# The second four tiles of a batch summed by ScalarE's accumulator in two of four periods

## What is computed

```python
cos = einsum('bhsd,bhtd->bhst', q, k)           # q, k with length 1
g = arccos(clip(cos, -1 + EPS, 1 - EPS))
score = (1 + g) ** -3.2
n_r, n_c = score.sum(-1), score.sum(-2)
k_tilde = score / n_r[..., None] / n_c[..., None, :]
out = (k_tilde / max(k_tilde.sum(-1), 1e-12)) @ v
```

## Time and profile before

| | us |
|---|---|
| median of 3 runs | 5188.83 (5183.14 to 5189.67) |
| the profiled execution | 5182.72 |
| its span, first to last instruction | 5181.0 |
| VectorE busy | 4095.3 |
| ScalarE busy | 4828.4 |
| TensorE busy | 3096.4 |
| GpSimd busy | 1904.3 |

### The profile page before, as it was taken

How to read it: one execution, slowest core, us unless ns; L and a number is a source line. 1 busy time by engine, 2 the same in 40 slices (tenths; PEclk the granted TensorE clock), 3 DMA queues, 4 the chain that set the end, 5 groups by cost and what they waited for, 6 DMA issues and landing times.

```text
span 5181.0 us, 37309 instructions
## 1 busy us (share of the span) xinstructions
PE 3096.4 (60%) x10590; PEld 798.7 (15%) x10590; DVE 4095.3 (79%) x4051; ACT 4828.4 (93%) x1248; POOL 1904.3 (37%) x629
## 2 busy tenths in 40 slices
PE   7555555555465545654566655665655565565799
PEld 4200111111010000100011111111111111111344
DVE  8777787877777777877788888888888888888577
ACT  5899999999999999999999999999999999999621
POOL 4433444334433444334433343334424442344000
PEclk9776657666766676567667778686877878787799
DMA  3100000000000000000000101010100101010200
GB/s 97 61 10 14 17 19 19 13 11 18 18 15 18 11 11 10 10 2 10 12 30 29 33 27 37 10 45 10 41 22 24 37 22 41 2 53 2 83 32 13
DMA packets 72049, 128.21 MB, mean 25 GB/s; under 512 B 9750, under 2 KB 47269, under 8 KB 71909
## 3 DMA queue, kind: packets, MB, share of 16 engines
q1 hardware_dynamic: 70757, 122.55, 7.6%
q0 software_dynamic: 1152, 4.19, 0.3%
HBM read 96.72 MB, written 29.88 MB: 24 GB/s over the span
## 4 chain that ended last, share of the span: by engine, by line
ACT 56%; issue 22%; DVE 11%; PE 7%; DVEq 1%; ACTq 0%; DMA 0%; SPq 0%
ACT X L1332 14%; ACT X L1305 13%; ACT X L1316 10%; ACT X L1324 9%; ACT X L1345 7%; DVE X L1092 4%; DVE ncol L1100 3%; PE psum L1561 3%; DVE rows L1197 1%; ACT L1316 1%; PE psum L959 1%; PE psum L974 1%; PE psum L933 1%; DVE X L1078 1%; PE psum L1526 0%
## 5 line engine op out<-in xcount | busy, mean ns | idle before, releaser
L1278 POOL TENSOR_TENSOR X<-X 128x2048 f32<-128x2048 f32 x504 | 1798.4, 3604 | 2803.0 <-DVE X L1078 2803.0
L933 PE MATMUL psum<-stacks 128*128 128x512 bf16 x4096 | 1672.0, 502 | 807.9 <-DVE X L1092 422.1
L1092 DVE TENSOR_TENSOR X<-psum,X 128x1024 f32<-128x1024 f32 x1024 | 1191.7, 1218 | 419.4 <-ACT X L1316 386.2
L959 PE MATMUL psum<-X,vp 128*32 128x512 f32 x4096 | 701.5, 848 | 1155.1 <-DVE vp L1106 1155.1
L1100 DVE TENSOR_REDUCE ncol<-X 128x4 f32<-128x8192 f32 x126 | 1094.0, 8683 | 364.4 <-ACT X L1345 362.7
L1078 DVE TENSOR_SCALAR X<-psum 128x1024 f32<-128x1024 f32 x1024 | 1191.3, 1217 | 30.6 <-DVE rows L1197 24.8
L1324 ACT ACTIVATE X<-X 128x4096 f32<-128x4096 f32 (+1 forms) x192 | 898.0, 4740 | 20.0 <-DVE X L1092 20.0
L1316 ACT ACTIVATE X<-X 128x4096 f32<-128x4096 f32 x256 | 904.8, 3605 | 0.7
L1332 ACT ACTIVATE X<-X,consts 128x16384 f32<-128x16384 f32 x64 | 892.9, 13951 | 0.8
L1305 ACT ACTIVATE X<-X,consts 128x8192 f32<-128x8192 f32 x126 | 889.7, 7108 | 0.2 <-issue 0.2
L1345 ACT ACTIVATE X<-X 128x8192 f32<-128x8192 f32 x126 | 878.9, 7022 | 2.0
(11 more groups left out here) (175 smaller groups left out, 1188.9 us busy)
## 6 DMA issues: line engine op xcount, KB each, us to landing
V<-expert_w SPq DMA_DIRECT2D x64, 512.0 KB, 3.6
stacks<-qk_parts SPq DMA_DIRECT2D x256, 64.0 KB
qk_parts<-X SPq DMA_DIRECT2D x96, 128.0 KB, 2.1
stacks<-qk_parts SPq DMA_DIRECT2D x64, 192.0 KB
head_out<-evac SPq DMA_DIRECT2D x32, 256.0 KB, 2.1
expert_w<-u_t SPq DMA_DIRECT2D x17, 256.0 KB, 2.6
X<-in_L_attn_x_dram POOLq DMA_DIRECT2D x8, 512.0 KB, 5.4
stacks<-qk_parts SPq DMA_DIRECT2D x32, 128.0 KB
```

What stands on the lines that cost most here:

```text
L933: return nc.tensor.matmul(dst, stacks[:, 1, buf, keys:keys + P], stacks[:, 0, buf, q0:q0 + n], start=True, stop=True)
L959: mm = nc.tensor.matmul(ps_sum[32 * j:32 * j + 32, :], vp[:, i, :], X[:, m % 2, i, j * 512:(j + 1) * 512], start=(m % 2 == 0 and i == 0), ...
L1092: nc.vector.tensor_tensor(part, ps_cos[j % 2], part, ALU.mult).then_inc(cos_ok, 1)
L1278: nc.gpsimd.tensor_tensor(own, own, own, ALU.mult).then_inc(square_ok, 1)
```

## The change

For batches in the tail with m = 0 or 3, the second piece (tiles 4 to 7) is handled like the last batch: ScalarE does four exps of one tile each with `accum_out` in place of one of four tiles, after a wait until both vp products of the batch before are made (so that `ncol` is free). VectorE leaves out the reduce_sum for that piece and only counts up its semaphore. `beside` is handed to `scores` and `values` for this. Fifteen batches are touched: m = 0 and 3 for k = 8 to 14, and m = 0 for k = 15.

```diff
--- before.py
+++ after.py
@@ -676,6 +676,10 @@
         EXP_PIECES = ((0, 4), (4, 8))
         LAST_PIECES = ((0, 4), (4, 7), (7, 8))
 
+        def summed(m, beside, piece):
+
+            return beside == "tail" and m in (0, 3) and piece == 1
+
         at[0] = (KC * NC * 2 - KC) * D
 
         den = carve([256])
@@ -1091,12 +1095,14 @@
                         part = X[:, m % 2, i, j * CW:(j + 1) * CW]
                         nc.vector.tensor_tensor(part, ps_cos[j % 2], part, ALU.mult).then_inc(cos_ok, 1)
 
-                def values(k, m, piece):
+                def values(k, m, piece, beside):
 
                     n = 4 * k + m
                     a, b = (LAST_PIECES if ends(k, m) else EXP_PIECES)[piece]
                     dve.wait_ge(score_ok, n * len(EXP_PIECES) + piece + 1)
-                    if not ends(k, m):
+                    if not ends(k, m) and summed(m, beside, piece):
+                        dve.sem_inc(sums_ok, 1)
+                    elif not ends(k, m):
                         nc.vector.reduce_sum(ncol[:, a:b], X[:, m % 2, a:b, :], AX.X).then_inc(sums_ok, 1)
                         dve.wait_ge(sums_ok, n * len(EXP_PIECES) + piece + 1)
 
@@ -1226,7 +1232,7 @@
                             side_gather(k, c, h)
                         todo = []
                     for piece in range(len(LAST_PIECES if ends(k, m) else EXP_PIECES)):
-                        values(k, m, piece)
+                        values(k, m, piece, beside)
                     if has(k, m + 1):
                         for i in range(BT):
                             mult(k, m + 1, i)
@@ -1323,7 +1329,7 @@
                         own = tiles(m, a, b)
                         nc.scalar.activation(own, own, ACT.Arctan).then_inc(atan_ok, 1)
 
-                def scores(k, m):
+                def scores(k, m, beside):
 
                     n = 4 * k + m
                     nc.scalar.preload_act_table_set("natural_log_exp_and_others")
@@ -1341,11 +1347,18 @@
                             ins.then_inc(score_ok, 1)
                         return
                     for piece, (a, b) in enumerate(EXP_PIECES):
+                        if summed(m, beside, piece):
+                            act.wait_ge(vp_ok, n * len(EXP_PIECES))
+                            for i in range(a, b):
+                                own = X[:, m % 2, i, :]
+                                ins = nc.scalar.activation(own, own, ACT.Exp, scale=POWER, accum_out=ncol[:, i:i + 1])
+                            ins.then_inc(score_ok, 1)
+                            continue
                         own = tiles(m, a, b)
                         nc.scalar.activation(own, own, ACT.Exp, scale=POWER).then_inc(score_ok, 1)
 
                 def emit(k, m, beside):
-                    scores(k, m)
+                    scores(k, m, beside)
                     if beside == "tail" and m == 1:
 
                         act.wait_ge(side_var, (k - SIDE + 1) * 2)
```

## The result

| | median us | runs | profiled execution, span |
|---|---|---|---|
| before | 5185.83 | 7 (5183.14 to 5189.67) | 5182.72, 5181.0 |
| changed | 5171.20 | 7 (5170.40 to 5172.71) | 5170.48, 5168.8 |

The changed kernel takes 0.9971 of the time of the kernel before (95% interval 0.9961 to 0.9981): about 15 us faster. 5175 was forecast, with a range of 5166 to 5189.

A forecast was written before the change was run, and what follows sets the result against it. ScalarE, 99% busy in the tail, was taken as the bound: 5182.7 - 20.0 (waits removed) + 9.8 (longer exps) = 5172.5 us, or 5178.6 from the median if its 6.1 us stay; forecast 5175, range 5166 to 5189.

The forecast's parts named there:

- ScalarE bounds the tail, and the time is its row plus the holes: Second half of the attention loop: ScalarE busy 99%, so time is its instructions plus 23.6 us of holes.
- The price, 15 x 0.65 = 9.8 us: Four summed one-tile exps replace one four-tile exp on ScalarE: 0.65 us longer in each of 15 batches.
- The estimate of 4.2 us: Price on ScalarE by the skill's figures alone: three more instructions cost 0.28 us a batch, 4.2 us in all.
- All 11 waits go, -20.0 us: ScalarE's arctan waits for VectorE's product 11 times in the tail, 20.0 us in total; all were to go.
- TensorE's adds as the next link, with 1.2 us to spare: After the change TensorE's eight adds hold VectorE's products; the eighth product ends 1.2 us before the sigmoids' end.
- VectorE less late behind m = 0: Batch 56: VectorE 1.2 us less late, its first reduction starting 13.0 us after the exps instead of 14.15.
- The wait on vp_ok costs nothing, GpSimd and the end of the loop don't bind: ScalarE's added wait met 40 us early; GpSimd's squares have 9 us left; TensorE's final side products move with ScalarE.
- The median: Shown median 6.1 us above the profiled execution: 5172.5 us if those are such waits, 5178.6 if from other stages.
- Rival A: VectorE's lateness stays through its first reduction and TensorE's adds; ScalarE pays 9.8 and keeps 20 us: 5192.5; chance 0.08.
- B: Rival: half the gain, as new waits come in later batches and 10 us of wait remain: 5182.5 us; chance 0.17.
- C: Rival: more gained, with the price on ScalarE near its lower bound of 4.4 us: 5167.1 us; chance 0.05.
- D: Rival: no visible effect, all waits gone but ScalarE's price at its upper 20.9 us: 5183.6 us; chance 0.05.

The follow-up runs named there:

- unroll_before: The kernel before with the loop over k = 9 to 14 written out for VectorE alone; median 5163.81 us, ratio 0.9957, stretch 2257.57 us.

## Why the prediction was right

- **ScalarE bounds the tail, and the time is its row plus the holes.** Right: the stretch moved only with the two. Written out, the same change only costs.
- **The price, 15 x 0.65 = 9.8 us.** Right: +0.64 to +0.66 us in each of the 15 cycles against a cycle with no wait. The estimate of 4.2 us from the Trainium skill's figures ("ScalarE: Activation LUTs", section "What ACT_TABLE_LOAD costs"), which have no price for the read of the accumulator, is refuted by these cycles: with a read behind each, four exps took 7.57 us, four times the 1.893 us of one, so none of the overlap was left.
- **All 11 waits go, -20.0 us.** Right, and a little too small. The cycles got 21.3 us shorter through it: a wait also costs the overlap of about 0.1 us with the sigmoids ahead of it, at 11 places. Another 0.7 us went in the m = 1 cycles, which I hadn't counted and which has nothing to do with the waits. Together that is the difference between -10.2 and -12.24 us.
- **TensorE's adds as the next link, with 1.2 us to spare.** Wrong, without harm to the sum. I had 12.8 us for the eight adds, at the slow pace throughout; they took 10.05 and 8.89 us, as the second half ran at a clock of 1.00. They ended before the first product or within 0.1 us of its start in every changed batch. VectorE's wait ahead of the products was for the first sigmoids (10.12 us in batch 56), never for TensorE, and what was to spare was the 0.8 to 1.1 us from the eighth product to the end of the sigmoids.
- **VectorE less late behind m = 0.** It didn't come so, and here was luck. Its first reduction started 13.5 us after the exps in batch 56 (13.0 forecast), but 14.0 to 15.7 in the four others that had a wait (14.0 to 14.2 before). At 15.7 us in batch 48 the adds as I had them would have ended at 15.7 + 9.5 + 12.9 = 38.1 us, 1.5 past the 36.59 from which arctan waits. They ended at 33.7. A slip besides: the 0.6 us that I said would stay at batch 56 with the old offsets is 0, since the sigmoids' end moves by 0.65 us too.
- **The wait on vp_ok costs nothing, GpSimd and the end of the loop don't bind.** Right: no such wait is listed, and the end has moved along.
- **The median.** I left open whether the 6.1 us between the profiled execution and the first three medians were more waits of this kind. The ratio over seven runs, 0.9971, is nearer to that reading, but its interval (10 to 20 us) holds the other as well.
- **Rival A** (price without gain), beside which stood the Trainium skill's rule that additions belong on VectorE ("ScalarE: Activation LUTs", section "Rules for kernel authors"). As a forecast it fell, since VectorE was late in front of a full ScalarE. As advice it holds: unroll_before, which leaves every sum on VectorE and takes the lateness away, has a stretch 9.0 us shorter than the changed kernel. B, C and D fell with the waits and the price measured.

What the forecast didn't see is why VectorE was late. I named the 3.4 us at the loop's return and built nothing on them. So the sum was right, term by term, while the path I gave for the time after the change (through TensorE's adds) was not.

## What to carry to other kernels

When the bounding engine waits for one that has slack in total, look for where that one is late, and make its delay short before giving its work to the bound: here the same waits went at no cost to ScalarE by writing VectorE's loop out, and for 0.19 us a batch by moving one tile instead of four. What an edit costs on the bounding engine is paid in every pass; what it gains ends with the last wait. Against a run-to-run spread of several us, cycle lengths of the bounding engine tell the terms apart to 0.02 us.

## What the runs showed of the chip that I had not expected

- VectorE's return in the loop cost 3.4 us between its last side work and the next reduction (3.1 to 5.5 us over the kernels here), while ScalarE's own return didn't show: its row ran on without a hole.
- In the loop body VectorE lost 0.3 us at each clip behind a gather, 24.8 us in all, and nothing there when written out.
- TensorE's second four adds took 3.61 us at a granted clock of 1.00 in all 15 batches in which they followed the first four at once, and 5.15 to 6.45 us at 0.56 to 0.70 in the 11 batches before in which it had stood 2.7 to 4.4 us between them and arctan waited.
- TensorE's four adds took 3.64 us at a granted clock of 1.00 and 6.32 us at 0.54, in two periods of one kernel, and with them a wait of ScalarE's, two engines further on, went from 0.34 to 3.73 us.
